# Attention's row scaling moved one item later in VectorE's order, and first weight slabs loaded one stage earlier, in a transformer layer on eight cores

## What is computed

```python
q = (x @ Wq)   # 16 heads of 128
k = (x @ Wk)   # 4 heads of 128
v = (x @ Wv)
# key j is visible to query i for i-512 < j <= i
scores = where(visible, q k^T / 128, -inf)
attn = softmax(scores) @ v @ Wo
x = layernorm(x + attn)            # over 2048 features
Wg, Wu, Wd = (w - 128) * scale[:, None]   # 8192 x 2048, 8192 x 2048, 2048 x 8192, int32 values 0..255
x = layernorm(x + (silu(x @ Wg.T) * (x @ Wu.T)) @ Wd.T)
```

## Time and profile before

| | |
|---|---|
| median of 3 runs | 2478.1 us (lowest 2476.18) |
| profiled execution, its own time | 2477.34 us |
| its span, slowest core (core 6) | 2475.8 us (cores 2463.6 to 2475.8) |
| TensorE busy | 2092.5 us (85%) |
| VectorE, ScalarE, GpSimd busy | 482.9 (20%), 337.4 (14%), 113.1 us (5%) |
| chain that ended last, TensorE's share | 76%, of it L695, L595, L603 18% each |
| median from issue to landing | gate 5.0, up 7.0, down 7.9, Wo 5.0 us |

### The profile page before, as it was taken

One profiled execution on the slowest core, in us unless ns is written; L12 is line 12 of the kernel. 1 busy time (PEld: TensorE's weight loads), 2 busy tenths in 40 slices (PEclk: granted clock), 3 DMA queues, 4 the chain that ended last, 5 costly groups with the idle time before them and its releaser, 6 DMA issues.

```text
span 2475.8 us, 23891 instructions; the slowest of 8 cores (2463.6 to 2475.8 us)
## 1 busy us (share of the span) xinstructions
PE 2092.5 (85%) x9624; PEld 932.9 (38%) x9624; DVE 482.9 (20%) x800; ACT 337.4 (14%) x606; POOL 113.1 (5%) x217
## 2 busy tenths in 40 slices
PE   0689766666899189999999999899999999999970
PEld 0334344444441034444443444344444443444310
DVE  0111166666110701010110000000101010000015
ACT  0000055555003310101010000010010100000030
POOL 1000000000000000000000000000000000000000
PEclk9999865665899589999999999999999999999985
DMA  9344200000330043434342333334443432333003
GB/s 226 47 68 68 56 1 1 1 1 1 69 68 0 0 85 69 85 69 85 69 85 43 62 66 68 57 70 79 73 80 72 82 69 51 68 68 68 17 0 136
DMA packets 31920, 147.65 MB, mean 60 GB/s; under 512 B 3907, under 2 KB 6085, under 8 KB 27078
## 3 DMA queue, kind: packets, MB, share of 16 engines
q0 software_dynamic: 30800, 127.94, 28.8%
q1 hardware_dynamic: 1014, 18.20, 2.1%
HBM read 265.66 MB, written 8.39 MB: 111 GB/s over the span
## 4 chain that ended last, share of the span: by engine, by line
PE 76%; DVE 9%; issue 5%; another core or an unknown queue 3%; ACT 2%; DMA 2%; DVEq 0%; ACTq 0%; POOL 0%; POOLq 0%; SPq 0%
PE psD L695 18%; PE psG L595 18%; PE psU L603 18%; PE psQ L198 5%; PE psW L407 4%; DVE sc L331 4%; PE psD L691 3%; PE psS L467 2%; PE psS L441 2%; DVE S_sb L530 1%; ACT ab L358 1%; DVE S_sb L535 1%; PE psQ L207 1%; PE psH L661 1%
## 5 line engine op out<-in xcount | busy, mean ns | idle before, releaser
L595 PE MATMUL psG<-ab 128*128 128x512 bf16 x2048 | 458.2, 382 | 57.9 <-DMA ab<-wu_is 57.9
L695 PE MATMUL psD<-ab 128*128 128x512 bf16 x2048 | 457.4, 382 | 0.0
L603 PE MATMUL psU<-ab 128*128 128x512 bf16 x2048 | 452.5, 379 | 0.0
L595 PEld LDWEIGHTS psG<-ab 128*128 128x128 bf16 x2048 | 201.8, 99 | 305.2 <-issue 67.5
L695 PEld LDWEIGHTS psD<-ab 128*128 128x128 bf16 x2048 | 196.2, 98 | 279.0 <-issue 54.9
L603 PEld LDWEIGHTS psU<-ab 128*128 128x128 bf16 x2048 | 200.2, 98 | 241.8
L615 DVE SCALAR_TENSOR_TENSOR ab<-psU,scl_sb,sq_sb 128x512 bf16<-128x512 f32 x128 | 90.2, 746 | 822.8 <-PE psU L603 822.8
L630 ACT ACTIVATE sq_sb<-psG,scl_sb 128x512 f32<-128x512 f32 x128 | 88.0, 687 | 774.3 <-PE psG L595 774.3
L305 PE MATMUL pT<-Dm_sb,ab 128*128 128x128 bf16 x640 | 82.6, 287 | 104.1 <-ACT ab L365 101.9
L705 DVE SCALAR_TENSOR_TENSOR S_sb<-psD,scl_sb,S_sb 128x1024 f32<-128x1024 f32 x32 | 41.1, 1284 | 483.1 <-PE psD L695 483.1
L198 PE MATMUL psQ<-ab 128*128 128x512 bf16 x512 | 113.6, 386 | 8.7 <-DMA ab<-wq_os 8.7
(11 more groups left out here) (71 smaller groups left out, 968.3 us busy)
## 6 DMA issues: line engine op xcount, KB each, us to landing
ab<-wg_is POOLq DMA_DIRECT2D x64, 512.0 KB, 5.0
ab<-wu_is POOLq DMA_DIRECT2D x64, 512.0 KB, 7.0
ab<-wd_os POOLq DMA_DIRECT2D x32, 1024.0 KB, 7.9
ab<-wq_os POOLq DMA_DIRECT2D x16, 512.0 KB, 5.0
ab<-wo_os POOLq DMA_DIRECT2D x16, 512.0 KB, 5.0
ab<-x_all POOLq DMA_DIRECT2D x1, 6144.0 KB, 66.9
ab<-wv_ks POOLq DMA_DIRECT2D x16, 128.0 KB, 68.8
ab<-wk_os POOLq DMA_DIRECT2D x4, 512.0 KB, 5.6
```

The source lines that it names most:

```text
L595: last = t.matmul(psG[i % 2][:, 512 * tt:512 * tt + 512], abv(wgu_o + 4096 * (i % 2) + 128 * k, 128), abv(y1_o + 1024 * k + 512 * tt, 512) ...
L603: last = t.matmul(psU[i % 2][:, 512 * tt:512 * tt + 512], abv(wgu_o + 4096 * (i % 2) + 2048 + 128 * k, 128), abv(y1_o + 1024 * k + 512 * t ...
L695: last = t.matmul(psD[o % 2][:, 512 * tt:512 * tt + 512], abv(wd_o + 4096 * (o % 2) + 128 * i, 128), abv(h_o + 1024 * i + 512 * tt, 512), ...
```

## The change

1. Attention, VectorE: step n now does mask add n, cast n-3, and then reciprocal and `Dm` of item n-1 instead of item n. TensorE's and ScalarE's orders are unchanged. The per-step blocks are merged into one block for each engine, and the counts that they wait for are worked out ahead.
2. Every weight load goes through `wdma`, which first waits until all earlier loads on its semaphore have landed. In the FFN the gate slab of a pair now counts on `we` and the up slab on `wo`; TensorE waits for both.
3. The first two Wo slabs are loaded at the start of attention; the first two gate/up pairs of the first half behind the LayerNorm; those of the second half at the start of the first half's down phase; the first two down slabs of a half at the start of its gate/up phase.
4. The output goes out in 16 DMAs, each with a wait for its own chunk's last VectorE operation, behind LayerNorm's barrier as before.

```diff
+        def wdma(g, pn, dst, src):
+            g.wait_ge(sems[pn], cnt[pn])
+            return inc(g.dma_start(dst, src), pn, 16)
...
+            @block.vector
+            def _(v):
+                for n in range(NIT + 3):
                     if n < NIT:
...
                     if 0 <= n - 3 < NIT:
...
-                    if n < NIT:
-                        v.wait_ge(ss, c_exp[n])
-                        c_rec[n] = inc(v.reciprocal(sums_sb[:, 2 * (n % 3) + 1:2 * (n % 3) + 2],
...
+                    if 0 <= n - 1 < NIT:
+                        m = n - 1
+                        v.wait_ge(ss, c_exp[m])
+                        assert inc(v.reciprocal(sums_sb[:, 2 * (m % 3) + 1:2 * (m % 3) + 2],
...
+            pre_wo = {}
+
+            @block.gpsimd
+            def _(g):
+                g.wait_ge(tm, tm0_attn)
+                for o in range(2):
+                    pn = "we" if o % 2 == 0 else "wo"
+                    pre_wo[o] = wdma(g, pn, abv(wbuf_o + 2048 * (o % 2), 2048), wo_os[o, :, :])
...
         emit_ln(write_bf16_to=y1_o)
...
+        @block.gpsimd
+        def _(g):
+            for i in range(2):
+                e = wdma(g, "we", abv(wgu_o + 4096 * (i % 2), 2048), wg_is[i, :, :])
+                o_ = wdma(g, "wo", abv(wgu_o + 4096 * (i % 2) + 2048, 2048), wu_is[i, :, :])
+                pre_gu[(0, i)] = (e, o_)
...
+                @block.gpsimd
+                def _(g, half=half):
+                    for o in range(2):
+                        pn = "we" if o % 2 == 0 else "wo"
+                        pre_wd[(half, o)] = wdma(g, pn, abv(wd_o + 4096 * (o % 2), 4096),
+                                                 wd_os[half, o, :, :])
...
-                        inc(g.dma_start(abv(wgu_o + 4096 * (i % 2), 2048), wg_is[ii, :, :]), pn, 16)
-                        inc(g.dma_start(abv(wgu_o + 4096 * (i % 2) + 2048, 2048), wu_is[ii, :, :]), pn, 16)
+                            wdma(g, "we", abv(wgu_o + 4096 * (i % 2), 2048), wg_is[ii, :, :])
+                            wdma(g, "wo", abv(wgu_o + 4096 * (i % 2) + 2048, 2048), wu_is[ii, :, :])
...
-                        t.wait_ge(we if i % 2 == 0 else wo, ld)
+                        t.wait_ge(we, ld[0])
+                        t.wait_ge(wo, ld[1])
...
+                if half == 0:
+                    @block.gpsimd
+                    def _(g):
+                        for i in range(2):
+                            e = wdma(g, "we", abv(wgu_o + 4096 * (i % 2), 2048), wg_is[32 + i, :, :])
+                            o_ = wdma(g, "wo", abv(wgu_o + 4096 * (i % 2) + 2048, 2048), wu_is[32 + i, :, :])
+                            pre_gu[(1, i)] = (e, o_)
...
-            sy.wait_ge(vv, cnt["vv"])
-            inc(sy.dma_start(y_out[:, :], S_sb[:, :]), "so", 16)
+            for k in range(KC):
+                sy.wait_ge(vv, ln2_done[k])
+                inc(sy.dma_start(y_out[:, 1024 * k:1024 * k + 1024],
+                                 S_sb[:, 1024 * k:1024 * k + 1024]), "so", 16)
```

More of the change, by code:

```diff
@@ L266, in build_nc, with _ @@
             ss0_attn = cnt["ss"]
+            tm0_attn = cnt["tm"]
+            vv0_attn = cnt["vv"]
             c_mm = [None] * NIT
+            c_tD = [None] * NIT
+            c_pv = [None] * NIT
             c_msk = [None] * NIT
+            c_ae = [None] * NIT
+            c_rec = [None] * NIT
+            c_D = [None] * NIT
             c_exp = [None] * NIT
             c_pTe = [None] * NIT
-            _ss = ss0_attn
+            _t, _v, _s = tm0_attn, vv0_attn, ss0_attn
+            for n in range(NIT + 3):
+                if n < NIT:
+                    _t += 1; c_mm[n] = _t
+                if 0 <= n - 2 < NIT:
+                    _t += 1; c_tD[n - 2] = _t
+                if 0 <= n - 3 < NIT:
+                    _t += 1; c_pv[n - 3] = _t
+                if n < NIT:
+                    _v += 1; c_msk[n] = _v
+                if 0 <= n - 3 < NIT:
+                    _v += 1; c_ae[n - 3] = _v
+                if 0 <= n - 1 < NIT:
+                    _v += 1; c_rec[n - 1] = _v
+                    _v += 1; c_D[n - 1] = _v
             for n in range(NIT + 2):
                 if n < NIT:
-                    _ss += 1
-                    c_exp[n] = _ss
+                    _s += 1; c_exp[n] = _s
                 if 0 <= n - 2 < NIT:
[L277 to L287, removed]
+                    _s += 1; c_pTe[n - 2] = _s
+            @block.tensor
+            def _(t):
+                for n in range(NIT + 3):
                     if n < NIT:
@@ L295, in _ @@
                         t.matmul(sc[:, 0:512], abv(qs, 128), abv(ks, 512), start=True, stop=True)
-                        c_mm[n] = inc(t.matmul(sc[:, 512:640], abv(qs, 128), abv(ks + 512, 128),
-                                               start=True, stop=True), "tm")
+                        assert inc(t.matmul(sc[:, 512:640], abv(qs, 128), abv(ks + 512, 128),
+                                            start=True, stop=True), "tm") == c_mm[n]
                     if 0 <= n - 2 < NIT:
@@ L321, in _ @@
                                             start=(b == 0), stop=(b == 4))
-                        c_pv[m] = inc(last, "tm")
-                @block.vector
-                def _(v, n=n):
+                        assert inc(last, "tm") == c_pv[m]
+            @block.vector
+            def _(v):
+                for n in range(NIT + 3):
                     if n < NIT:
```

74 lines of the change are left out of this document (40 added, 34 removed).

## The result

The changed kernel takes 2452.5 us (median of 10 runs, 2450.2 to 2474.3), against 2478.4 us for the kernel before (median of 10). The ratio is 0.9911 with a 95% interval of 0.9887 to 0.9935, so the change saves 22 us, 16 to 28 by that interval (the medians lie 25.8 apart): real, and too small to count as faster by 2%. The forecast was 2442 with a range of 2414 to 2464. Most terms held; the largest, attention, gave 12.6 us where 21 stood. The profiled execution took 2451.8 (span 2450.2 on core 2; the cores lie between 2437.4 and 2450.2).

The account below looks back on a forecast made before the run. Attention was taken as bound by a 2.41 us ring through VectorE and ScalarE, with waits for weights at the seams. Terms -21 - 6.1 + 1.5 - 1.0 - 7.6 - 2.5 + 0 + 0.5 = -36.2 gave 2442, range 2414 to 2464.

Parts of the forecast that it names:

- Attention, -21: Attention loop: mask adds come 2.26 us apart on average instead of 2.42, saving 21 us with a shorter first wait.
- Dm to transposes 0.50: Attention loop: TensorE's transposes start 0.50 us after VectorE's Dm starts.
- ring A: Attention, one item: Dm, transposes, product, VectorE's cast, reciprocal, back to Dm; 2.31 us at half clock, 1.81 at full.
- h: Attention, VectorE: hand-over from the start of the product's cast to the reciprocal, taken as 0.21 us, bounds 0 and 0.45.
- Full clock in attention, 14%: Rival: TensorE is granted 2.4 GHz most of attention, -48 us in place of -21, 2415 us; chance 0.14.
- Attention gains nothing, 9%: Rival: cast-to-reciprocal hand-over near 0.45, a new ring replaces the old; +6 to 0 us, 2463 to 2469; chance 0.09.
- Mask collision, +1.5: Start of attention: the early Wo loads collide with the mask load, costing 1.5 us, ends 0 and +4.
- First half, -1.0: Seam into first FFN half: prefetch leaves no earlier, but the first pair travels alone; -1.0 us, ends 0 and -2.9.
- Second half, -7.6 and -2.5: Seam into second FFN half: early gate/up loads save 7.6 us of pause, and 2.5 more by holding full clock.
- crowded-prefetch rival: FFN: down loads delay gate/up pair 2 by some 6 us in each half; +12 us, 2454; chance 0.05.
- Output, +0.5: Kernel end: sixteen stores leave no earlier than one, issue costs 0.37 each and runs ahead of the data; +0.5 us.
- rival of 42 us: Kernel end: each of the sixteen stores waits out its fixed part in series; +42 us, 2483; chance 0.05.

Follow-up runs that it names:

- experiment 1: Changed kernel with VectorE's reciprocal and Dm put back to item n in step n; merged blocks, early loads and 16 stores stay: 2463.2 us, ratio 0.9941.
- experiment 6: Kernel before, with the 512-column scores matmul in attention issued twice: 2478.0 us (one run).
- experiment 5: Changed kernel with the 512-column scores matmul in attention issued twice, same result: 2417.4 us, ratio 0.9758.
- experiments 4: Changed kernel with VectorE's step reordered: mask add n, reciprocal and Dm of n-1, only then the cast of product n-3: 2384.2 us, ratio 0.9618.
- experiment 10: Changed kernel with GpSimd holding the two early Wo loads until the masks have landed: 2447.3 us, ratio 0.9889.
- experiment 8: Changed kernel with the first two gate/up pairs issued before the first LayerNorm instead of behind its barrier: 2444.3 us, ratio 0.9864.
- Experiment 9: Changed kernel with one output store again instead of sixteen: 2452.1 us, ratio 0.9898.
- experiment 3: Changed kernel with TensorE's two waits before the transposes exchanged, ScalarE's cast first and Dm last: 2449.3 us, ratio 0.9885.
- experiment 7: Changed kernel without the barrier at the end of the last LayerNorm, each store waiting for its own part: 2435.1 us, ratio 0.9827.

## Why the prediction was right or wrong

**What bound the kernel before: right.** VectorE's order closed the ring of 2.41; experiment 1 restores it with nothing else undone, and experiment 6 shows that TensorE's speed is not in it.

**Attention, -21: too large, measured -12.6** (first to last mask add, 308.8 to 296.2). The step that failed is "Dm to transposes 0.50", taken from the only row where the transposes waited for Dm alone. In the loop they also wait for ScalarE's cast, and then it is 0.60: ring A is 2.40, not 2.31. The prediction remarked that the row had one wait and did not ask what a second one costs, and no row of before could tell it, since there the cast came last. All other steps held: h was 0.21 (taken 0.21, ends 0 and 0.45), the products 0.49 and 0.84, and at full clock 0.28 and 0.55. What was gained: from the third mask add (312.99) to the last the mean period is 2.34 ((605.24 - 312.99) / 125) against 2.42, through the items at full clock (granted 0.63), and that is 10.6; the other 2 lie at the start, where the third mask add comes 3.9 after the first instead of 6.0. Put 2.40 in the forecast's own sum, 0.8 x 2.40 + 0.2 x 2.04 = 2.33, and 0.09 x 127 gives attention about -12 and the kernel 2451: that one number accounts for 9 of the 10.5 us between forecast and result. That it comes so near is partly luck. The sum's picture of full-clock items 2.04 apart did not appear: they came 1.9 apart (ring A at full clock, 0.60 + 0.28 + 0.55 + 0.21 + 0.25), each followed by a longer one, and with the measured grant of 0.63 in place of 0.60 the same sum would give -14.

**Full clock in attention, 14%: did not come, but its price was right.** It was forecast at 2415, and experiment 5, which brings it about, has 2417.4. The Trainium skill ("TensorE: Matmul & The Clock Gate", The HAM clock gate) says that activity releases the slow clock. The traces agree in kind: the surplus matmuls raised the grant from 0.63 to 0.97 (experiment 5) and from 0.60 to 0.88 (experiment 6). The rule was cited as a reason why denser attention could hold the clock; it did so in experiments 4 and 5, not in the change as made.

**Attention gains nothing, 9%.** Wrong in its cause (h was not 0.45), yet close in effect at half clock: 2.40 against 2.42.

**Seam into Wo, -6.1: measured -6.2.** **Mask collision, +1.5: +3.1** on the slowest core, inside the ends of 0 and +4; experiment 10 shows the cause.

**First half, -1.0: -0.3.** GpSimd issues behind LayerNorm's barrier, as said, so nothing is early; experiment 8 shows what the barrier cost, 8 us. From GpSimd's issue to the first matmul takes 7.6 to 10.5 by core before and 7.6 to 9.6 now, 9.0 and 8.4 on average, so the -0.3 of the two slowest cores says little about what the first pair gains by travelling alone.

**Second half, -7.6 and -2.5: -7.7 and -3.0** (32 matmuls at 0.22 are 7.0, before 9.99). The clock held through the pause of 1.97.

**Down weights, 0: right.** Pair 2's gate load left at 876.33, after 7.31 of waiting for a down load on GpSimd, and TensorE never stopped. The crowded-prefetch rival did not show.

**Output, +0.5: about +2.7** in the trace (25.5 against 22.8; +2.4 by the medians over the cores). The sentence "Issue costs 0.37 each and runs ahead of the data" was wrong: sixteen took 17.2 us. The rival of 42 us was further off: with the issues spread over 17.2 us, the last store's landing took 7.8, and the fixed part was not paid sixteen times. The Trainium skill's 2.0 us fixed per DMA ("DMA: Bandwidth & Descriptors", Anatomy of one DMA) is given there for DMAs issued by GpSimd, and these stores are SyncE's; if it holds for them, it was overlapped here. Experiment 9 against the change puts the cost of splitting at 2 to 4 us in all.

The terms as measured: -12.6 + 3.1 - 6.2 - 0.3 - 10.7 + 2.7 = -24.0; the spans of the profiled executions differ by 25.6 and the medians by 25.8. The 1.6 to 1.8 left over is small beside the 13 us between the fastest and slowest core.

## What to carry to other kernels

When an order moves, write down every new ring with its hand-overs, and take each hand-over from a row with the same number of waits as the new place will have; one 0.10 us in a loop of 128 was most of the error here. Ask next which operation stands in front of the one that others wait for: moving the scaling ahead of the cast as well, one operation further, was worth 68 us more than the change. A prefetch or a split store behind a barrier gains nothing until the barrier goes.

## What had not been expected of the hardware

When TensorE waits for two semaphores ahead of its transposes, they start 0.50 us after the start of VectorE's Dm (0.35 long) if that is the late one and its wait is written last, and 0.60 if it is written first; behind the start of ScalarE's cast (0.68 long) it is 0.83 and 0.93 (the change and experiment 3). Only TensorE's transposes were looked at.

Issuing 128 surplus matmuls of 512 columns made the changed kernel 35 us faster, because TensorE was then granted 2.4 GHz for nearly all of attention and two rings pass through it. What the runs show is the granted clock that went with each loop: 0.60 before and 0.88 with the surplus there, 0.63 in the change and 0.97 with the surplus, 0.95 with the period at 1.83. What the chip asks for, they do not show.

SyncE's issue of a 512 KB store took 1.08 us on average when sixteen were in a row, and 0.35 (median) in experiment 7, where each waited for its chunk and they left some 1.1 us apart. So it is not the store itself that takes long to issue; whether the queue or the data ahead of it holds it back stays open.
